# Four graph layers on one core: the hops' weights applied to the rows before the sweeps, in place of after them

## The chip, the core and the metric

The kernel runs on one core of one Trainium2 chip. The metric is the device time of one execution in microseconds; the kernel before has a median of 759.16 us over three runs (756.97 to 760.65). All work of a run is in one program: TensorE (PE, with its weight loads shown apart as PEld), VectorE (DVE), ScalarE (ACT), GpSimd (POOL) and SyncE (SP, which only issues transfers here).

## The reference

x is 4096 x 64, adj is a dense 4096 x 4096 float32 matrix (64 MB) that is mostly zero. Four layers are applied one after another, each as x = x + layer(h) with h = relu(layernorm(x)):

```
layer 0:  1 - 0.1 h - 0.01 sum(h * (adj @ h), axis=1)
layer 1:  two hops: for k in 0, 1:  y = tanh(concat([adj @ y, y], 1) @ W[k])      (y starts as h, W[k] is 128 x 64)
layer 2:  mask = adj != 0; rank = cumsum(mask, 1); only the last 100 nonzeros of a row count,
          each weighted with 0.5 ** (its distance from the end);  w @ (h @ weight) + bias
layer 3:  tanh([h, t] @ W1 + b1) @ W2 + b2 + adj @ (h B^T) - rowsum(adj) * (h B^T)
```

A hop's argument of tanh is `(adj @ y) @ Wa + y @ Wx`, with Wa and Wx the upper and lower 64 rows of W[k]. It equals `adj @ (y @ Wa) + y @ Wx`, so that Wa can be applied on either side of the product with adj.

## The kernel before

adj has to be walked five times: sweep L0 (layer 0), L1A and L1B (the two hops), L2 (layer 2) and L3 (layer 3). A sweep has 8 chunks of 512 output rows (`W`), and a chunk has 16 blocks b of 256 adj columns (`TQ` = 2 tiles of 128), so a block is 128 x 1024 float32. Blocks travel in pairs of 1 MB: pair k holds blocks 2k and 2k+1. Pairs 0 and 4 of every chunk (and pair 2 of chunk 4) are kept in SBUF (`cache`) after L0; the others go through four landing slots (`land`). SP issues the loads in program order on one queue; a load waits until every engine that reads the slot's last pair is done with it. L1A and L2 walk the chunks backwards (`ch`), so a sweep begins with the chunk whose pairs are still in the slots.

In L0, L1A, L1B and L3 the two tiles of a block are multiplied as two 64-column halves into `accA` (L1157), with the transposed layer input as the weights: `X[0]` in L0, L1B, L3, and `X[1]` in L1A. The accumulated chunk is thus 2 x 64 rows (two partial sums, one above the other) by 512. In L0, DVE also makes the mask of each block (L979) and PE counts the nonzeros of each tile per output row (`count`, L1172), because L2 needs for every tile the number of nonzeros behind it. In L1A and L1B, DVE adds blocks into `totals` (L957, L961) for the row sums of layer 3, on the blocks in `TOTALS`. In L2 the masks go through a triangle matmul (L1189), ACT and, in block 6, DVE turn the result into weights (L484, L482), and PE multiplies them with the rows (L1200).

The rest of the work of a chunk (its epilogue, in numbered stages) is put between the blocks of the next chunk. Each engine runs the same loop: block b, then the stages whose place is b (`stages_after`). Places come from `STAGES_L1B`, `ROW_STAGES`, and `QUICK` for the first chunk of a sweep; in L0 and L1A stage b//2 stands at odd b. All queues are in order: a stage that waits holds up everything behind it on its engine. What the change touches:

- Epilogue of a hop (L1A, L1B): stage 0 transposes the four tiles of the hop's own rows (PE L1047, ACT L705 to `rowsT`); stage 1 copies `accA` to `accS` (ACT L739), and PE multiplies `rowsT` by Wx (L1081, `wx0`, `wx1`) and `accS` by Wa (L1085, `wagg0`, `wagg1`) into `nat`; stage 3 takes the tanh from PSUM (ACT L745 to `X[0]`, or L749 to `natS`).
- L1B's epilogue then goes on as the others do: rows added (DVE L927), the norm (DVE L841, L842, L847, L848, POOL L641, L634, L644, DVE L860), a transpose of the normed rows `hS` (PE L1047), and layer 2's product (L1106). PE also adds up `totals` (L1074).
- L0's epilogue: join of the two halves (L1093), row products on DVE (L885, L887), the new x (L893, L896), the norm into `X[1]` (stage 7, L860).
- Counts and left-over weights in L0: a tile's last row (`LAST` = 127) is left out of the triangle and is handled apart. ACT copies the upper half of the counts (L785), DVE adds the lower (L908) and fits in the last rows of adj (L913), which SP has loaded (`left_adjacency`, L515, issued behind the eight loads of the next chunk); ACT makes the weights (L792) and stores both.

Of the kernel before, what the change touches and what calls it, by code (L numbers as in the profile page):

```python
# [15 lines left out]
P = 128  # L16
N = 4096
D = 64
# [120 lines left out]
for _name, _n in (("wagg0", D), ("wx0", P), ("wagg1", D), ("wx1", P), ("l2w", P), ("bT", P), ("w1t", 2),  # L139
                  ("b1", 2), ("t", 1), ("bias", D), ("ident", P), ("join", D), ("ones", 1), ("full", 1),  # L140
                  ("w1", 256), ("w2", 2 * D), ("b2", D)):
    COLS[_name] = (_at, _at + _n)
    _at += _n
# [23 lines left out]
def tr_no(p, c, i=0):  # L167

    return {L1A: c, L1B: 8 + 2 * c + i, L2: 24 + c, L3: 32 + c}[p]
# [13 lines left out]
def totalled_no(p, c, b):  # L183
# [3 lines left out]
    return (first - 1) * c + at - 1 if p == L1A else (first - 1) * NC + second * c + at  # L187

# [29 lines left out]
def evac_no(c, b):  # L218

    on_dve = sum(k in EVAC_DVE for k in range(NQ))  # L220
    if b in EVAC_DVE:
# [5 lines left out]
HT_PE = {L1B: "turn", L2: 7}  # L227
HT_ACT = {L1B: "turned", L2: 7}
# [3 lines left out]
STAGES_L1B = {0: 1, 1: 3, 3: 7, 4: 8, 5: 10, "turn": 12, "turned": 13, 6: 15, 7: 15}  # L232

QUICK = {L1A: {0: 0, 1: 1, 3: 4, 4: 5, 5: 6, 6: 7, 7: 9}, L1B: {0: 0, 1: 1, 3: 4},
         L2: {3: 2, 4: 3, 5: 5, "turn": 8, "turned": 9, 6: 11, 7: 11, 8: 12},
# [5 lines left out]
def stages_after(p, c, b, before, before2):  # L241
# [9 lines left out]
    if p == L1B:  # L251
        return at_block({8: 2}, before2) if before2 and b == 2 else at_block(STAGES_L1B, before)
    found = []
# [33 lines left out]
def gnn_kernel(nc, x_in, adj_in, left_in_d, wts_in, tri_in, out):  # L287
# [3 lines left out]
    left_d = nc.dram_tensor("left_weights", (NC, 2 * NT, W), U16, kind="Internal").ap()  # L291
    hT_d = nc.dram_tensor("rows_transposed", (NC, P, 2 * P), F32, kind="Internal").ap()
    counts_d = nc.dram_tensor("counts", (NC, 2 * NT, W), BF16, kind="Internal").ap()
# [3 lines left out]
    with ExitStack() as ctx:  # L297
# [17 lines left out]
        later = sb("later", [P, 4 * NT], BF16)  # L315
        loS = sb("loS", [2 * NT, P], F16)
        lowS = sb("lowS", [2 * NT, 2 * W], U16)
# [50 lines left out]
        sums_p = nat[:, CH:CH + 4]  # L368
# [28 lines left out]
        left_rows, cleared = sem("left_rows"), sem("cleared")  # L397
# [64 lines left out]

        def rows4(t):
# [9 lines left out]
        def weights_out(eng, ops, c, b):  # L473
# [16 lines left out]
        def _(sp):  # L490
# [4 lines left out]
            tile_counts = counts_d.rearrange("c (t k) w -> c t k w", k=2)  # L495

            def counts_for(g):
# [3 lines left out]
                else:  # L501
# [4 lines left out]
                             tile_counts[ch(L2, c), 4 * k:4 * k + 4, 0].rearrange("(o t) w -> o t w", o=1))\  # L506
                    .then_inc(counts_in[g % (MASKS // 2)], 16)

            def left_adjacency(c):

                if c:
                    sp.wait_ge(left_later, c)
                else:
                    sp.wait_ge(cleared, 1)
                sp.dma_start(loadjS[1:2 * NT:2, :], left_in_d[:, c * W:(c + 1) * W]).then_inc(left_adj, 16)  # L515
# [7 lines left out]
            def left_rows_of(c):  # L523

                sp.wait_ge(cleared, 1)
                sp.wait_ge(copy_used, copied_no(L1B, c, 1) + 1)
                for t in range(4 * c, 4 * c + 4):
                    sp.dma_start(loS[2 * t + 1:2 * t + 2, :], tile16(t)[LAST:P, :]).then_inc(left_rows, 16)
# [102 lines left out]
        def _(pool):  # L631
# [56 lines left out]
            nc.gpsimd.memset(loS[:, :], 0.0)  # L688
            nc.gpsimd.memset(loadjS, 0.0).then_inc(cleared, 1)
# [4 lines left out]
        def _(act):  # L694
# [12 lines left out]
            def epilogue(at, e):  # L707
# [11 lines left out]
                if at == 0 and p in (L1A, L1B):  # L719

                    act.wait_ge(tr_done, tr_no(p, c, 0) + 1)
# [584 lines left out]
```

## Time and profile before

| | |
|---|---|
| median of 3 runs | 759.16 us (756.97 to 760.65) |
| the profiled execution | 757.24 us |
| its span, first to last instruction | 755.4 us |
| around the span | 1.8 us |
| granted TensorE clock, mean | 0.995 |
| PE, DVE, ACT, POOL busy | 93%, 58%, 25%, 14% of the span |
| moved by DMA | 262.58 MB, mean 348 GB/s |
| PE on sweep blocks (L1157) | 499 us in 2048 instructions |

A float32 product shows as two matmul instructions, so a block is 4 instructions of L1157. The matmuls of a stretch overlap: the mean of one (601 ns) says less than the distance from the start of one row of the timeline to the start of the next. In the timeline a sweep's chunk can be told by the copy of `accA` (L739, in L2 L737), one for each chunk. By these copies L0 takes from about 20 to 184 us, L1A to 319, L1B to 460, L2 to 614 and L3 to the end.

### The profile page before, as it was taken

What the parts mean: (1) busy time and instruction counts of PE and PEld (TensorE: products, weight loads), DVE (VectorE), ACT (ScalarE), POOL (GpSimd) and SP (SyncE); (2) the same over time, 40 slices, a digit from 0 to 9 for tenths busy, and PEclk for the clock granted to TensorE, in tenths of its full rate; (3) what the DMA queues carried; (4) which work ended last, traced back from release to release, by engine and by line L of the source; (5) the groups of instructions that cost most, each with busy time, mean ns of one, the idle gap of its engine ahead of it and who ended that gap; (6) DMA issues with size and microseconds to landing.
All of it is one profiled execution on the core that took longest, in us unless ns stands there. A gap on an engine that the chain in (4) does not pass through costs nothing. (4 is left out here: it accounts for less than half of the span.)

```text
span 755.4 us, 10059 instructions
## 1 busy us (share of the span) xinstructions
PE 703.3 (93%) x3656; PEld 280.1 (37%) x3656; DVE 438.7 (58%) x757; ACT 191.0 (25%) x279; POOL 104.8 (14%) x126
## 2 busy tenths in 40 slices
PE   1899999998999999999999997899999999999997
PEld 0333333333333333444444443344444433333332
DVE  5776776777888877846666556577777730000000
ACT  2010111110100000101111114688888842000100
POOL 5011011111100000002221222011111121211210
PEclk9999999999999999999999999999999999999999
DMA  9999999996699999699998986699899849999994
GB/s 370 379 365 412 416 420 414 413 412 249 232 406 401 333 382 374 261 376 369 374 367 311 363 329 224 220 356 394 302 379 375 331 143 362 369 413 399 363 385 159
DMA packets 49680, 262.58 MB, mean 348 GB/s; under 512 B 6880, under 2 KB 18912, under 8 KB 19296
## 3 DMA queue, kind: packets, MB, share of 16 engines
q1 hardware_dynamic: 39136, 252.51, 85.9%
q10 hardware_dynamic: 10496, 9.44, 4.0%
q8 instruction: 29, 0.48, 0.2%
q14 instruction: 19, 0.16, 0.1%
HBM read 255.76 MB, written 6.16 MB: 347 GB/s over the span
## 5 line engine op out<-in xcount | busy, mean ns | idle before, releaser
L1157 PE MATMUL accA<-land,X 128*64 128x512 f32 x1504 | 364.7, 601 | 8.9 <-DMA land<-adj_blocks 7.3
L1157 PEld LDWEIGHTS accA<-land,X 128*64 128x64 f32 x1504 | 100.4, 137 | 185.6 <-issue 138.9
L979 DVE TENSOR_SCALAR uS<-land 128x1024 bf16<-128x1024 f32 (+1 forms) x188 | 126.9, 723 | 42.6 <-DMA land<-adj_blocks 36.7
L961 DVE TENSOR_TENSOR uS<-uS,land 128x512 f32<-128x512 f32 x186 | 130.6, 702 | 34.7 <-DMA land<-adj_blocks 25.1
L1157 PE MATMUL accA<-cache,X 128*64 128x512 f32 x544 | 134.3, 605 | 16.5 <-DVE X L1012 12.6
L484 ACT ACTIVATE wS<-spare 128x1024 uint16<-128x1024 f32 x120 | 115.3, 1031 | 18.8 <-PE spare L1189 18.0
L1189 PE MATMUL spare<-uS,triA 128*128 128x512 bf16 x256 | 76.4, 380 | 10.4 <-DMA uS<-counts 3.8
L641 POOL TENSOR_TENSOR hS<-tS 128x256 f32<-128x256 f32 x24 | 21.2, 883 | 422.4 <-DVE tS L842 422.4
L1200 PE MATMUL accA<-wS,X 128*128 128x512 bf16 x256 | 76.3, 380 | 0.0
L945 DVE TENSOR_TENSOR tS<-uS,nat 128x256 f32<-128x256 f32 x8 | 3.4, 421 | 123.8 <-PE nat L1089 123.8
L1157 PEld LDWEIGHTS accA<-cache,X 128*64 128x64 f32 x544 | 38.9, 139 | 91.7 <-issue 84.7
L705 ACT ACTIVATE rowsT<-tr 128x256 f32<-128x256 f32 x32 | 12.3, 383 | 202.5 <-PE tr L1047 202.4
L1172 PE MATMUL spare<-uS,later 128*64 128x512 bf16 x256 | 50.0, 383 | 4.8 <-DVE uS L979 4.8
L979 DVE TENSOR_SCALAR uS<-cache 128x1024 bf16<-128x1024 f32 (+1 forms) x68 | 44.1, 687 | 7.7 <-DMA cache<-adj_blocks 5.1
L739 ACT ACTIVATE accS<-accA 128x512 f32<-128x512 f32 x32 | 19.1, 597 | 115.5 <-PE accA L1157 106.9
L961 DVE TENSOR_TENSOR uS<-uS,cache 128x512 f32<-128x512 f32 x54 | 37.7, 699 | 3.4
L1189 PEld LDWEIGHTS spare<-uS,triA 128*128 128x128 bf16 x256 | 20.1, 99 | 45.5 <-issue 27.0
L1200 PEld LDWEIGHTS accA<-wS,X 128*128 128x128 f16 x256 | 24.9, 97 | 30.6 <-issue 0.7
L634 POOL TENSOR_TENSOR rstd<-var,power 128x4 f32<-128x4 f32 (+1 forms) x25 | 29.7, 1189 | 38.7 <-DVE var L848 38.7
L792 ACT ACTIVATE wS<-wS,wts 64x512 uint16<-64x512 bf16 x8 | 5.8, 722 | 109.6 <-DVE wS L913 109.6
L1172 PEld LDWEIGHTS spare<-uS,later 128*64 128x64 bf16 x256 | 15.4, 111 | 43.2 <-issue 26.0
L482 DVE TENSOR_SCALAR wS<-spare 128x1024 uint16<-128x1024 f32 x8 | 9.8, 1224 | 23.0 <-PE spare L1189 23.0
(85 smaller groups left out, 392.5 us busy)
## 6 DMA issues: line engine op xcount, KB each, us to landing
land<-adj_blocks SPq DMA_DIRECT2D x219, 1024.0 KB, 7.4
cache<-adj_blocks SPq DMA_DIRECT2D x17, 1024.0 KB, 13.6
xin<-x_rows ACTq DMA_DIRECT2D x32, 128.0 KB, 7.6
x_rows<-zS ACTq DMA_DIRECT2D x24, 128.0 KB, 5.8
cache<-x_rows SPq DMA_DIRECT2D x1, 1024.0 KB, 4.9
uS<-counts SPq DMA_DIRECT2D x64, 4.0 KB
out_rows<-zS ACTq DMA_DIRECT2D x8, 128.0 KB, 6.7
rows_transposed<-rowsT SPq DMA_DIRECT2D x7, 128.0 KB, 7.8
```

The source lines that it names most:

```text
L482: ops.tensor_scalar(w, of, 0.0, None, ALU.max).then_inc(w_ready_dve, 1)
L484: ops.activation(w, of, ACT.Relu).then_inc(w_ready, 1)
L634: nc.gpsimd.tensor_tensor(out[:, 0:ntile], of[:, 0:ntile], power[:, 0:ntile], ALU.pow)\
L641: nc.gpsimd.tensor_tensor(hS[:, :], tS[:, :], tS[:, :], ALU.mult).then_inc(rows_squared, 1)
L705: nc.scalar.activation(rowsT[:, :], tr[:, 0:2 * P], ACT.Copy).then_inc(tr_evac, 1)
L739: last = nc.scalar.activation(accS[:, :], accA[:, c % 2, :], ACT.Copy)
L961: nc.vector.tensor_tensor(total, total, of[:, i * W:(i + 1) * W], ALU.add)\
L979: nc.vector.tensor_scalar(masks(b)[0:rows, :], block_of(p, c, b)[0:rows, :], 0.0, None, ALU.not_equal)\
L1157: last = nc.tensor.matmul(accA[k * D:(k + 1) * D, c % 2, :], tile(X[p % 2], TQ * q + k), of[:, k * W:(k + 1) * W], start=(b == 0), stop=(b ...
L1172: last = nc.tensor.matmul(spare[k * D:(k + 1) * D, c % 2, :], later[:, 2 * (NT - t):2 * (2 * NT - t)], masks(b)[:, k * W:(k + 1) * W], sta ...
L1189: last = nc.tensor.matmul(spare[:, 2 * (b % 2) + k, :], triA[:, :], masks(b)[:, k * W:(k + 1) * W], start=True, stop=True)
L1200: last = nc.tensor.matmul(accA[:, c % 2, :], tile16(TQ * q + k), weights(n)[:, k * W:(k + 1) * W].bitcast(BF16), start=(b == 0 and k == 0) ...
```

## The change

1. A hop's weights are applied before its sweep. `wagg`, `wx` (64 and 128 columns) become one table `hop0`, `hop1` of [Wa, Wx]. After the norm of a chunk in L0 (and after the tanh in L1A) the new rows are transposed (stage "turn", PE; "turned", ACT) and multiplied by [Wa, Wx] (stage "hop", PE, 4 products with 64 rows of contraction and 128 columns, into banks 2 and 3 of `spare`). ACT copies y @ Wa to `X[1]` or `X[0]`, which the sweep multiplies with adj, and y @ Wx to `Z` (stage "hopped"); `Z` lies in the space of the layer-2 weights `wS`.
2. After a hop's sweep PE only transposes `accS` (4 transposes, as L3 does); DVE adds the two halves and `Z` (stage "added", 2 operations of 128x256), and ACT takes the tanh from SBUF (stage "tanh").
3. Counts: the count matmul keeps its two column halves. ACT copies all 128 partitions as bf16 (stage "part"), one matmul adds the halves ("stack"), DVE copies 32 rows ("counts"), ACT makes the left-over weights for 32 rows ("weights", with the counts' store), DVE multiplies them by `adj != 0` of the last rows ("left"), ACT stores them ("left out"). Both stores are 32 rows, where they were 64, and the zeroed buffers on POOL go.
4. Places: L0 and L1A have tables of their own, `STAGES_L0` and `STAGES_L1A`. Entering L1A, the norm of L0's last chunk stands at blocks 1 to 6 (it stood at 4 to 9), ahead of most of the adding of row sums.
5. The weights of layer 2 in the first four blocks wait until the part of `Z` that they overwrite has been read.

The core of the diff:

```
-def tr_no(p, c, i=0):
-
-    return {L1A: c, L1B: 8 + 2 * c + i, L2: 24 + c, L3: 32 + c}[p]
+def tr_no(p, c):
+
+    return {L0: c, L1A: 8 + c, L1B: 16 + c, L2: 24 + c}[p]
...
-QUICK = {L1A: {0: 0, 1: 1, 3: 4, 4: 5, 5: 6, 6: 7, 7: 9}, L1B: {0: 0, 1: 1, 3: 4},
-         L2: {3: 2, 4: 3, 5: 5, "turn": 8, "turned": 9, 6: 11, 7: 11, 8: 12},
+STAGES_L0 = {0: 1, 1: 2, "part": 3, 3: 5, "stack": 5, "counts": 6, 4: 7, 5: 8, "weights": 8, 6: 10, "left": 10, 7: 11,
+             "left out": 12, "turn": 13, "turned": 13, "hop": 14, "hopped": 15}
+STAGES_L1A = {1: 2, "added": 4, "tanh": 6, "turn": 8, "turned": 9, "hop": 11, "hopped": 13}
+STAGES_L1B = {0: 1, 1: 3, "added": 5, "tanh": 6, 3: 7, 4: 8, 5: 10, "turn": 12, "turned": 13, 6: 15, 7: 15}
+QUICK = {L1A: {0: 0, 1: 1, 3: 1, 4: 1, 5: 2, 6: 4, 7: 6, "turn": 10, "turned": 10, "hop": 11, "hopped": 12, "part": 13,
+               "stack": 14, "counts": 14, "weights": 14, "left": 15, "left out": 15},
+         L1B: {1: 1, "added": 2, "tanh": 3, "turn": 5, "turned": 5, "hop": 7, "hopped": 8},
+         L2: {"added": 0, "tanh": 0, 3: 2, 4: 3, 5: 5, "turn": 8, "turned": 9, 6: 11, 7: 11, 8: 12},
```

The new stage on PE:

```
+                if at == "hop":
+
+                    pe.wait_ge(tr_evac, tr_no(p, c) + 1)
+                    if hop_no(p, c):
+                        pe.wait_ge(hop_evac, 2 * hop_no(p, c))
+                    for t in (0, 2, 1, 3):
+                        half = (t // 2 * D, t // 2 * D + D)
+                        last = nc.tensor.matmul(spare[:, 2 + t // 2, t % 2 * P:(t % 2 + 1) * P],
+                                                rows_t(t % 2)[half[0]:half[1], :],
+                                                wt("hop0" if p == L0 else "hop1", rows=half), start=True, stop=True)
+                    last.then_inc(hop_done, 1)
```

The new stage "added" on DVE, and what waits there for the last rows of adj:

```
+                def hop_added():
+
+                    if tanh_no(p, c):
+                        dve.wait_ge(tanh_done, tanh_no(p, c))
+                    dve.wait_ge(nat_done, nat_no(p, c, 0) + 1)
+                    dve.wait_ge(hop_evac, 2 * hop_no(p - 1, ch(p - 1, ch(p, c))) + 2)
+                    parts = nat[:, :].rearrange("p (t h d) -> p h t d", h=2, d=D)
+                    L(nc.vector.tensor_tensor(rows4(tS), rows4(chunk(Z, ch(p, c))), parts[:, 0], ALU.add))
+                    nc.vector.tensor_tensor(rows4(tS), rows4(tS), parts[:, 1], ALU.add).then_inc(nat_evac, 1)
+
...
+                    if at == "left":
                         dve.wait_ge(left_adj, 16 * (c + 1))
-                        dve.wait_ge(count_ready, c + 1)
+                        dve.wait_ge(left_most, c + 1)
```

How the order of the instructions moves, at the three places that matter below. First PE, one chunk of L1B (the second hop), from the last blocks of one chunk to the middle of the next. `tr` holds transposes, `nat` what is to go back to rows. Before:

```order
L1106 MATMUL nat<-wts,rowsT 128x2x64 x2
L1157 MATMUL accA<-land,X 64x512 x4
L1047 MATMUL tr<-wts,X 64x128 x4
L1157 MATMUL accA<-land,X 64x512 x4
L1074 MATMUL nat<-wts,uS 128x1 x4
L1081 MATMUL nat<-wts,rowsT 128x2x64 x2
L1085 MATMUL nat<-wts,accS 128x64 x4
```

After the change:

```order
L1141 MATMUL nat<-wts,rowsT 128x2x64 x2
L1207 MATMUL accA<-land,X 64x512 x8
L1115 MATMUL tr<-wts,uS 128x1 x4
L1122 MATMUL nat<-wts,accS 128x128 x4
L1207 MATMUL accA<-land,X 64x512 x4
```

The transposes of the hop's rows (L1047) and the two products by weights (L1081, L1085) are gone from this place; four transposes of `accS` (L1122) are there.

Second DVE, in L0, the second half of a chunk (uS<-land and uS<-cache are the masks of blocks; the first row of each piece is the mask of block 10 or 12). Before, the work on the left-over weights (L908, L913) stands behind the mask of block 15, the last of the chunk:

```order
L847 TENSOR_REDUCE st<-hS 128x4 [waits rows_squared]
L848 TENSOR_SCALAR var<-st 128x4 [waits link]
L979 TENSOR_SCALAR uS<-land 128x1024 [waits counted,landed2] x2
L860 TENSOR_SCALAR X<-tS 128x256 [waits rows_scaled]
L908 TENSOR_TENSOR wS<-wS,spare 64x512 [waits counts_out,count_half]
L913 SCALAR_TENSOR_TENSOR wS<-wS 64x512 [waits left_made,count_ready,left_adj]
```

After the change:

```order
L873 TENSOR_REDUCE st<-hS 128x4 [waits rows_squared]
L874 TENSOR_SCALAR var<-st 128x4 [waits link]
L954 SCALAR_TENSOR_TENSOR countS<-lowS,rowsT 32x512 [waits left_out,left_most,left_adj]
L1024 TENSOR_SCALAR uS<-land 128x1024 [waits counted,landed0]
L886 TENSOR_SCALAR hS<-tS 128x256 [waits rows_scaled]
L1024 TENSOR_SCALAR uS<-land 128x1024 [waits counted,landed1] x2
L1024 TENSOR_SCALAR uS<-land 128x1024 [waits counted,landed2] x2
```

The operation that waits for the last rows of adj (`left_adj`) now stands ahead of the masks of blocks 11 to 15.

Third ACT at the first blocks of L2 (L484 and L513 make the weights of a block). Before:

```order
L705 ACTIVATE rowsT<-tr 128x256 [waits nat_done,tr_done]
L739 ACTIVATE accS<-accA 128x512 [waits nat_done,swept]
L484 ACTIVATE wS<-spare 128x1024 [waits tri_done] x3
L749 ACTIVATE natS<-nat 128x256 [waits copy_used,nat_done]
L484 ACTIVATE wS<-spare 128x1024 [waits tri_done]
```

After the change:

```order
L740 DMA xin<-x_rows 128x256 [waits rows_out,copy_used]
L755 ACTIVATE accS<-accA 128x512 [waits nat_done,swept]
L513 ACTIVATE wS<-spare 128x1024 [waits nat_evac,tri_done]
L767 ACTIVATE natS<-tS 128x256 [waits copy_used,nat_evac]
L513 ACTIVATE wS<-spare 128x1024 [waits nat_evac,tri_done] x3
```

The copy of transposed rows (L705) is gone from here, and the tanh (L749, now L767) stands behind the weights of one block, where it stood behind those of three.

## Rows read from the trace of the kernel before

**Rows 1.** The page, part 1: busy us (share of the span) xinstructions

```profile
PE 703.3 (93%) x3656; PEld 280.1 (37%) x3656; DVE 438.7 (58%) x757; ACT 191.0 (25%) x279; POOL 104.8 (14%) x126
```

**Rows 2.** Windows: us, PE, PEld, DVE, ACT, POOL, clock, DMA share, GB/s

```profile
101.20:122.50 21.30, 19.63 (x104) 6.93 (x104) 15.22 (x28) 2.35 (x5) 2.55 (x3) 1.00 1.02 414
...
372.10:390.00 17.90, 17.90 (x106) 8.10 (x104) 10.99 (x20) 1.89 (x6) 3.81 (x5) 1.00 0.96 355
```

**Rows 3.** Timeline of PE in L1B: start us, us, engine, line, tile

```profile
374.05 0.69 PE L1081 MATMUL nat<-wts,rowsT 128*128 128x128 f32 x4
374.58 1.00 PE L1085 MATMUL nat<-wts,accS 128*128 128x64 f32 x8
375.51 1.94 PE L1157 MATMUL accA<-land,X 128*64 128x512 f32 x8
...
388.81 0.61 PE L1047 MATMUL tr<-wts,X 128*64 128x128 f32 x8
389.25 1.89 PE L1157 MATMUL accA<-land,X 128*64 128x512 f32 x8
```

**Rows 4.** Timeline of PE in L3

```profile
686.03 1.14 PE L1120 MATMUL spare<-wS 64*128 64x256 f32 x8
...
688.11 0.66 PE L1089 MATMUL nat<-wts,accS 128*128 128x128 f32 x4
688.69 1.94 PE L1157 MATMUL accA<-land,X 128*64 128x512 f32 x8
```

**Rows 5.** Timeline of ACT: the copies of accA, L1B and L3

```profile
353.84 0.61 ACT L739 ACTIVATE accS<-accA 128x512 f32<-128x512 f32 x1
...
443.78 0.60 ACT L739 ACTIVATE accS<-accA 128x512 f32<-128x512 f32 x1
...
649.96 0.60 ACT L739 ACTIVATE accS<-accA 128x512 f32<-128x512 f32 x1 [11.02 <-PE accA L1157]
...
750.82 0.60 ACT L739 ACTIVATE accS<-accA 128x512 f32<-128x512 f32 x1 [11.69 <-PE accA L1157]
```

**Rows 6.** SP's issue of the last rows of adj, and its time to landing

```profile
171.13 0.47 SPq L515 DMA_DIRECT2D wS<-adj_left  x1
...
DMA to landing us min/median/max: 10.3/10.3/10.3
```

**Rows 7.** Timeline of DVE in the last chunk of L0: masks of blocks 10, 11

```profile
175.79 1.29 DVE L979 TENSOR_SCALAR uS<-land 128x1024 bf16<-128x1024 f32 x2
```

**Rows 8.** DMA issues in a chunk of L0 (142:163) and of L3 (670:686)

```profile
land<-adj_blocks SPq DMA_DIRECT2D x6, 1024.0 KB, 11.3
...
land<-adj_blocks SPq DMA_DIRECT2D x6, 1024.0 KB, 8.0
```

**Rows 9.** Timeline of PE from L0 to the end of L1A's first chunk

```profile
183.57 1.89 PE L1157 MATMUL accA<-land,X 128*64 128x512 f32 x8
187.32 1.08 PE L1093 MATMUL nat<-wts,accS 128*128 128x64 f32 x8 [1.86 <-ACT accS L739]
...
195.22 7.04 PE L1157 MATMUL accA<-land,X 128*64 128x512 f32 x32
202.09 1.89 PE L1157 MATMUL accA<-cache,X 128*64 128x512 f32 x8
```

**Rows 10.** Windows after that wait: columns as in rows 2

```profile
190.00:192.00 2.00, 2.00 (x8) 0.73 (x6) 1.90 (x5) 0.00 (x0) 0.00 (x0) 0.50 0.27 92
```

**Rows 11.** Timeline of DVE: the last norm of L0, first and last operation

```profile
188.84 0.43 DVE L885 TENSOR_TENSOR tS<-X,natS 128x256 f32<-128x256 f32 x1 [0.60 <-ACT natS L749]
...
197.44 0.29 DVE L860 TENSOR_SCALAR X<-tS 128x256 f32<-128x256 f32 x1 [0.86 <-POOL tS L644]
```

**Rows 12.** Timelines of PE and DVE in the first chunk of L2

```profile
461.61 1.03 PE L1189 MATMUL spare<-uS,triA 128*128 128x512 bf16 x4
...
472.92 1.01 PE L1189 MATMUL spare<-uS,triA 128*128 128x512 bf16 x2 [3.62 <-DVE wS L482]
...
465.41 0.16 DVE L921 TENSOR_SCALAR rowsum<-nat 128x4 f32<-128x4 f32 x1 [4.92 <-ACT natS L749]
```

More of the change, by code:

```diff
@@ L187, in totalled_no, with hop_no, tanh_no @@
     return (first - 1) * c + at - 1 if p == L1A else (first - 1) * NC + second * c + at
+def hop_no(p, c):
+    return {L0: c, L1A: 8 + c}[p]
+def tanh_no(p, c):
+    return {L1A: c, L1B: 8 + c}[p]
 def row_no(p, c):
@@ L252, in stages_after @@
         return at_block({8: 2}, before2) if before2 and b == 2 else at_block(STAGES_L1B, before)
+    if p in (L0, L1A):
+        return at_block(STAGES_L0 if p == L0 else STAGES_L1A, before) if before else []
     found = []
@@ L741, in epilogue @@
                 if at == {L2: 2, L3: None}.get(p, 3):
[L742 to L746 removed]
+                    if p in (L0, L2):
+                        act.wait_ge(nat_done, nat_no(p, c, 0) + 1)
                         if copied_no(p, c):
                             act.wait_ge(copy_used, copied_no(p, c))
[L749 to L750 removed]
+                        nc.scalar.activation(natS[:, :], nat[:, 0:CH], ACT.Copy).then_inc(nat_evac, 1)
+                if at == "tanh":
+                    act.wait_ge(nat_evac, nat_no(p, c, 0) + 1)
+                    if p == L1B:
+                        act.wait_ge(copy_used, copied_no(p, c))
+                    nc.scalar.activation((hS if p == L1A else natS)[:, :], tS[:, :], ACT.Tanh).then_inc(tanh_done, 1)
+                if at == "hopped":
+                    act.wait_ge(hop_done, hop_no(p, c) + 1)
+                    for of, to in ((0, X[1] if p == L0 else X[0]), (1, Z)):
+                        nc.scalar.activation(chunk(to, ch(p, c)).rearrange("p (b t d) -> p b t d", b=2, d=D),
+                                             hop_out(of), ACT.Copy).then_inc(hop_evac, 1)
                 if at == HT_ACT.get(p, None):
@@ L754, in epilogue @@
                         act.wait_ge(hT_out, 16 * c)
-                    act.wait_ge(tr_done, tr_no(p, c, 1 if p == L1B else 0) + 1)
+                    act.wait_ge(tr_done, tr_no(p, c) + 1)
+                    if p in (L0, L1A):
+                        act.wait_ge(left_made, min(c + 1, NC - 1) if p == L0 else NC)
                     rows_transposed()
@@ L1052, in epilogue @@
                 p, c = e
-                if at == 0 and p in (L1A, L1B):
-                    tr_free(tr_no(p, c, 0))
-                    transposed(lambda j: tile(X[p % 2], 4 * ch(p, c) + j))
                 if p == L2 and at in ("join0", "join1") or p == L2 and c == NC - 1 and at == 1:
@@ L1286 @@
     put("ones", np.ones((P, 1), np.float32))
-    put("full", np.full((P, 1), NEIGH * BIT, np.float32))
+    put("full", np.full((P, 1), (NEIGH + 1) * BIT, np.float32))
     i, j = np.arange(P)[:, None], np.arange(P)[None, :]
```

170 lines of the change are left out of this document (83 added, 87 removed).

## The prediction

> **What bounds the kernel now.** I read the page first: PE is busy for 93% of the span, DVE for 58%, ACT for 25% [rows 1]. So each sweep is limited by PE or by the loads that it eats, and the windows by chunk tell which. In L0 a chunk takes 21.3 us with PE idle for 1.7 of them and DMA full at 414 GB/s: L0 goes at the pace of the loads. In L1B a chunk takes 17.9 us, PE has no gap at all, and DMA moves 355 GB/s, less than it has shown it can: L1B goes at the pace of PE [rows 2]. What is added to PE is thus free in L0 up to 1.7 us per chunk; what is taken from PE counts in L1B until the loads bind. The timelines at the borders between sweeps show where PE stands still: 1.86 us entering L1A [rows 9], with a granted clock of 0.50 some microseconds later [rows 10], and 3.62 us in L2's first chunk [rows 12].
>
> **L1B, per chunk.** Costs on PE are distances between starts. Removed: the transposes of the hop's rows, 0.44 us (388.81 to 389.25), the product by Wx, 0.53 (374.05 to 374.58), the product by Wa, 0.93 (374.58 to 375.51) [rows 3]: 1.90 us. Added: four transposes of `accS`, which L3 does already, 0.58 us (688.11 to 688.69) [rows 4]. Net -1.32 us. A chunk of L1B now takes (443.78 - 353.84) / 5 = 17.99 us, and would take 16.67 if PE alone counted. The nearest measure of the other bound is L3: nearly the same PE work, six loads of 1 MB and three transfers of 128 KB, (750.82 - 649.96) / 6 = 16.81 us [rows 5]; L1B has one transfer of 128 KB fewer. I take 16.75 for L1B, between the two, so 1.2 us saved. L1B's first chunk trades 1.90 us of L1A's old epilogue for the new one of L1A (below) and gains 0.1; its last chunk has few loads and gains the full 1.3. The seven chunks: 6 x 1.2 + 1.3 = 8.5 us saved. DVE's two new adds (0.42 us each, as its other operations of this size) and ACT's copies lie beside PE: DVE is busy for 11 of 17.9 us there [rows 2]. Without that cover they would cost 0.85 us per chunk.
>
> **L1A, per chunk.** Removed 1.90 us, added 0.58 (transposes of `accS`), 0.44 (transposes of the tanh's rows) and the hop's own products. Those have no row of their own. Nearest above: the hidden layer's products in L3, also with 64 rows of contraction and 128 columns of weights, but 256 columns wide, 1.14 us [rows 4]. Nearest below: the transposes, as many instructions of the same width, 0.44 us [rows 3]. I take 0.75, since the weights, which must be loaded in both, are as wide as in the row above. Sum +1.77 - 1.90 = -0.1 us; DVE gets 0.85 us more, and loads wait for DVE in this sweep. I count L1A as unchanged (-1 to +3 us over the sweep).
>
> By the Trainium skill (TensorEngine Tiling (Array Packing), Key Properties) a change of tiling mode drains TensorE. The sweeps run in column halves and the hop in row halves, so each hop is entered and left through a drain. The row of the hidden layer includes its own drains, and taken whole it would make the hop 0.4 us dearer, 3 us over L1A.
>
> **L0.** PE gets 0.44 + 0.75 us for turn and hop and about 0.3 for the stack: 1.5 of the 1.7 us that are free [rows 2]. Stores fall by 64 KB of about 8.8 MB per chunk, 0.15 us, 1 us in all. But DVE now waits for the last rows of adj behind block 10. In the last chunk SP issues them at 171.13, and they land 10.3 us later, at 181.4 [rows 6], since they stand behind the loads on SP's queue. DVE is done with block 10 at about 176.4 (two masks from 175.79) [rows 7]. So the mask of block 11 comes some 5 us later, in this chunk and in the like ones before it. Queued behind it are the norm and the masks of blocks 12 to 15, for which PE's counts wait, and both hold landing slots. While loads are the bound this costs little: a load now takes 11.3 us from issue to landing, so that four slots' worth are under way; held 3 us longer they take about 8, which is L3's figure [rows 8], at a like rate. I give it +2 us over seven chunks for slots that come back later, and with the saving +1 (bounds -1 and +8, the latter 1.2 us per chunk).
>
> **L0 to L1A.** Here the loads have ended and the 5 us show. Before, L1A begins at 183.57 [rows 9]. After, in the same clock: landing 181.4, the operation of 0.68 us and a mask of 0.69 make 182.8; then PE has the counts of blocks 11 to 15 and the sweeps of 13 to 15 (4 x 0.21 + 3 x 0.86, the last count after them), turn and hop with their switches (1.4), and is done at about 187.8: 4.2 us later. In L1A's first chunk PE gains the wait of 1.86 us for `accS` (ACT is free now when the sweep ends) and up to 1.8 us that the low clock took [rows 9, 10], and gets 1.5 us of turn, hop and stack. It also gets a wait: the norm on DVE took 8.6 us from natS on (188.84 to 197.7) with row sums between [rows 11]; with the norm put ahead it will still take about 8.5, since DVE and POOL alternate, and starts some 3 us into the chunk. PE reaches the turn behind block 10 after 11 x 0.86 + 1 = 10.5 us, the norm ends near 12: 1.4 us of wait. The chunk has 64 instructions of 0.215 us (6.87 us for 32) [rows 9], so 13.7, with 1.0 of joins, 0.2, 1.5, switches 0.3, wait 1.4: 18.1 us, against 202.09 - 183.57 = 18.5. DVE, which got less done by then, ends its row sums a little later still. Border: +4 us (-2 to +6).
>
> **L1B to L2.** PE comes to the first triangle (461.61) about 1.0 us sooner: `accS` no longer waits for the copy of the transposed rows, and 1.3 us of work are gone. DVE now waits 4.92 us for the tanh, up to 465.41, because it stands behind three weight copies on ACT [rows 12]. With the adds done at about 461.6 and one weight copy ahead of it, the tanh ends at about 463.0: 2.5 us sooner. The norm, the weights of block 6 on DVE and the triangle of block 8 (472.92) move up by the same 2.5 us. What is late next is the same chain, shifted. -2.5 us, -4 if the shorter stall keeps the clock up. L2's later chunks and L3 are untouched.
>
> **Sum**, against the profiled execution (757.24 us, 1.8 of them around its span): -8.5 (L1B), -0.1, +1 (L0), +4 (border), 0 (L1A), -2.5 (L2) = -6 us: 751.2. The median of the runs is 1.9 us above the profiled execution, so I forecast 753 us.
>
> **Rivals.**
> - The wait on the last rows of adj is no wait: they land with the reduced queue well before, or PE catches up. For it: the shorter the queue, the sooner a small transfer lands. Against it: they stand behind pair 7 in program order, which is needed at 18 us of a chunk's 21.3. Then the border costs nothing and may even gain the 1.86 us and the clock: 753 - 6 = 747. Chance 0.22.
> - L1B runs into the loads at once, and drains around the hops cost PE in L1A. For it: DMA share 0.96 in L1B [rows 2]. Against it: L3's 16.81 us. With 17.2 us for L1B (355 GB/s at a share of 0.96 is 370 at 1.00, by which the 6.55 MB of six loads and two transfers of 128 KB take 17.7; I take the middle of that and 16.67) the gain is 6 instead of 8.5, and L1A loses 3: 758. Chance 0.22.
> - It gets slower: in L0 the stall on DVE closes a loop. The slots of blocks 10 and on come back later, pair 7 is issued later, and the last rows behind it land later. PE work from the wait to the next issue of pair 7 is some 13.5 us (four blocks, turn, hop, six blocks with join), and the loop holds the chunk as soon as the landing takes over 7.8 us, or as soon as the one long gap lowers PE's clock as in [rows 10]. At 1.5 us per chunk and the border at +5.5 us: 753 + 9.5 + 1.5 = 764. Chance 0.14.
> - The forecast itself: 0.42, its own range 749 to 757.
>
> **How the numbers follow.** A change of about 0.5% (3.8 us) is what a measurement of this kernel can tell from none; 755.4 is the border. Faster: 0.36 of the forecast, all of the first rival, a little of the second: 0.60. Same: the rest of the forecast and most of the second: 0.25. Slower: 0.15. The range reaches down to the first rival with its clock gain, 745, and up to short of the third, 761.
>
> **What will show it.** Copies of `accA` in L1B 16.7 us apart, in L1A as now. The hop's products 0.75 us. In L0 an idle of 4 to 5 us on DVE ahead of the "left" operation, put down to adj_left, chunks of 21.3 to 21.6 us, and L1A beginning some 5 us late. PE's wait for DVE in L2's first chunk 1.5 to 2 us in place of 3.62. I am wrong if "left" shows no wait, if chunks of L0 grow past 22.3 us, or if L1B stays above 17.2.

## The result: slower by 0.8%, with the profile after

The changed kernel takes 765.51 us (median of eight runs) against 761.18 us for the kernel before in the same set of runs, a ratio of 1.0076, 95% interval 1.0051 to 1.0102. The ratios here compare the fast runs of a set only, and they are estimates that differ from the quotient of the two medians beside them (1.0057 for this pair). `changed_again`, the same kernel in the set of the first experiments, gave 767.37 against 760.17 us, 1.0116 (1.0081 to 1.0150). The forecast was 753 us and faster. The profiled execution took 767.67 us with a span of 765.8 us, 10.4 us more than before. The first part of its page shows PE with 1.9 us more of busy time [rows 1], so on balance most of the 10.4 us is waiting:

```profile
PE 705.2 (92%) x3664; PEld 274.3 (36%) x3664; DVE 452.0 (59%) x789; ACT 203.6 (27%) x311; POOL 104.3 (14%) x124
```

The starts of the sweeps on PE, read from both timelines, say where it went:

| stretch | before, us | after, us | difference | forecast |
|---|---|---|---|---|
| start to the first block of L1A | 183.57 | 196.63 | +13.1 | +1 in L0 and +4.2 at its end |
| L1A | 133.6 | 137.9 | +4.3 | -0.5 |
| L1B, to the first triangle of L2 | 144.4 | 138.2 | -6.2 | -9.5 |
| L2, to the first copy in L3 | 175.6 | 175.0 | -0.6 | -1.5 |
| L3 | 118.2 | 118.1 | -0.1 | 0 |

Two thirds of what the change was to give back in L1B came; L0 took twice as much. In L0 the chunks are longer, all but one. The windows of the changed kernel from copy to copy of `accA` (columns as in rows 2):

```profile
61.20:83.42 22.22, 20.27 (x123) 8.12 (x121) 15.00 (x29) 3.34 (x7) 2.62 (x3) 1.00 1.01 395
83.42:107.52 24.10, 21.96 (x123) 8.82 (x121) 15.42 (x30) 3.34 (x7) 2.62 (x3) 0.93 1.00 404
107.52:128.38 20.86, 20.36 (x124) 8.12 (x122) 14.23 (x28) 3.34 (x8) 3.11 (x3) 1.00 1.00 397
128.38:152.29 23.91, 21.95 (x123) 8.82 (x121) 15.36 (x29) 3.33 (x7) 2.61 (x3) 0.93 0.98 375
152.29:174.12 21.83, 20.27 (x124) 8.13 (x121) 14.64 (x28) 3.34 (x8) 2.62 (x3) 1.00 0.97 375
```

There are three kinds of chunk: one of 20.86 us, in which PE is nearly never idle; those of about 22 us, in which PE is busy for the same 20.3 us and idle for nearly 2; and those of 24 us, in which the granted clock of 0.93 is added, and with it 1.7 us more of busy time. Before, a chunk was 21.3 us at 414 GB/s [rows 2]; here the 22 and 24 us ones move 375 to 404. So L0 no longer goes at the pace of the loads. The waits of DVE and of PE between 57 and 186 us, as total, times and longest, say on what:

```profile
PE spare L1222 <- DVE uS L1024: 8.1, 5, 2.1
...
DVE tS L923 <- ACT natS L762: 16.4, 6, 3.8
DVE countS L948 <- PE spare L1157: 10.0, 6, 1.7
DVE countS L954 <- DMA lowS<-adj_left: 8.2, 4, 2.3
DVE uS L1024 <- DMA land<-adj_blocks: 5.4, 4, 1.7
```

Before, PE did not wait for DVE at all in this stretch, and DVE waited for hardly anything but loads (27.8 us for `land`, 5.1 for `cache`, and 2.6 us in two short waits for PE and POOL). Now DVE's waits for loads have shrunk to 5.4 us for `land` and 1.2 for `cache`, which is to say that it is the late one, and PE's counts (L1222) wait 8.1 us for its masks (L1024). One turn of it in the timelines of DVE, of PE and of SP's queue:

```profile
144.45 0.68 DVE L954 SCALAR_TENSOR_TENSOR countS<-lowS,rowsT 32x512 uint16<-32x512 f32 x1 [2.10 <-DMA lowS<-adj_left]
145.16 0.69 DVE L1024 TENSOR_SCALAR uS<-land 128x1024 bf16<-128x1024 f32 x1
...
145.91 0.41 PE L1222 MATMUL spare<-uS,later 128*64 128x512 bf16 x2 [1.96 <-DVE uS L1024]
146.15 1.72 PE L1207 MATMUL accA<-land,X 128*64 128x512 f32 x4
...
136.38 0.42 SPq L540 DMA_DIRECT2D lowS<-adj_left  x1
...
160.30 0.42 SPq L540 DMA_DIRECT2D lowS<-adj_left  x1
```

SP asks for the last rows of adj at 136.38, they land at 144.4, DVE has stood for 2.10 us, the mask behind the product (L954) is late, PE waits 1.96 us for it, and the next four matmuls, which mostly take 1.03 us, take 1.72. The next request of SP, which stands behind loads whose slots PE and DVE give back, goes out at 160.30.

### The profile page after: what moved, and what is told of

Same layout as the page of the kernel before. It is cut to its first block and busy times, and to the rows that moved or that the text cites. A ratio compares the mean times of both kernels' runs of the same rounds, so it can differ in the third digit from the quotient of the medians.

```text
span 765.8 us, 10173 instructions
## 1 busy us (share of the span) xinstructions
PE 705.2 (92%) x3664; PEld 274.3 (36%) x3664; DVE 452.0 (59%) x789; ACT 203.6 (27%) x311; POOL 104.3 (14%) x124
## 5 line engine op out<-in xcount | busy, mean ns | idle before, releaser
L1207 PE MATMUL accA<-land,X 128*64 128x512 f32 x1504 | 369.7, 607 | 7.3 <-DMA land<-adj_blocks 7.1
L1006 DVE TENSOR_TENSOR uS<-uS,land 128x512 f32<-128x512 f32 x186 | 133.0, 715 | 29.3 <-DMA land<-adj_blocks 20.5
L1024 DVE TENSOR_SCALAR uS<-land 128x1024 bf16<-128x1024 f32 (+1 forms) x188 | 127.5, 721 | 18.9 <-DMA land<-adj_blocks 12.5
L513 ACT ACTIVATE wS<-spare 128x1024 uint16<-128x1024 f32 x120 | 115.1, 1031 | 16.8 <-PE spare L1239 16.0
L665 POOL TENSOR_TENSOR hS<-tS 128x256 f32<-128x256 f32 x24 | 23.5, 979 | 460.0 <-DVE tS L868 460.0
L1222 PE MATMUL spare<-uS,later 128*64 128x512 bf16 x256 | 50.6, 391 | 16.7 <-DVE uS L1024 16.7
L1024 DVE TENSOR_SCALAR uS<-cache 128x1024 bf16<-128x1024 f32 (+1 forms) x68 | 44.6, 686 | 1.8 <-DMA cache<-adj_blocks 1.2
L1222 PEld LDWEIGHTS spare<-uS,later 128*64 128x64 bf16 x256 | 15.3, 113 | 61.9 <-DVE uS L1024 37.8
L1092 PE MATMUL tr<-wts,hS 128*64 128x128 f32 x256 | 21.5, 290 | 4.4 <-DVE hS L886 4.1
L1092 PEld LDWEIGHTS tr<-wts,hS 128*64 128x64 f32 x256 | 16.4, 145 | 21.9 <-issue 21.6
```

What stands on the lines that cost most here:

```text
L513: ops.activation(w, of, ACT.Relu).then_inc(w_ready, 1)
L665: nc.gpsimd.tensor_tensor(hS[:, :], tS[:, :], tS[:, :], ALU.mult).then_inc(rows_squared, 1)
L1006: nc.vector.tensor_tensor(total, total, of[:, i * W:(i + 1) * W], ALU.add)\
L1024: nc.vector.tensor_scalar(masks(b)[0:rows, :], block_of(p, c, b)[0:rows, :], 0.0, None, ALU.not_equal)\
L1092: last = nc.tensor.matmul(tr[half:half + D, (j % 2) * P:(j % 2 + 1) * P], of(j), wt("ident"), start=True, stop=True)
L1207: last = nc.tensor.matmul(accA[k * D:(k + 1) * D, c % 2, :], tile(X[p % 2], TQ * q + k), of[:, k * W:(k + 1) * W], start=(b == 0), stop=(b ...
```

## The experiments

The changed kernel was timed once more, unedited, beside the first three experiments as their measure:

> The changed kernel as it is, as the yardstick for the others of this call. It was 0.8% above the kernel before (about +6 us). Every theory expects the same again, 1.005 to 1.010.

Its 1.0116 is above, a little over the 1.005 to 1.010 expected, and its L0 shows the same: PE waits 9.1 us for DVE's masks between 57 and 186 us, DVE 9.5 us for the last rows of adj.

**The wait is a loop: the rows asked for three loads earlier, and one load later.** `left_early` moves SP's request from behind the eighth load of a chunk in L0 to behind the fifth; nothing else.

```diff
-                    for cc, k in L0_LOADS[c * PAIRS:(c + 1) * PAIRS]:
+                    for i, (cc, k) in enumerate(L0_LOADS[c * PAIRS:(c + 1) * PAIRS]):
+                        if c and i == 5:
+                            left_adjacency(c - 1)
...
-                    if c:
-                        left_adjacency(c - 1)
```

> One edit: in the first sweep SP issues the last rows of adj behind five of the chunk's eight loads, not behind all eight. Theory A (the wait of DVE for these rows, which stand last in the queue, closes a loop: landing, masks 11 to 15, PE, slots, pair 7, landing; its one long gap also lowers PE's clock): the wait on DVE vanishes, chunks of the first sweep fall from 22.5 to 21.3 to 21.6 us, the first hop begins 2 us sooner after the last load; 8 to 11 us less than the changed kernel, 3 to 5 us under the kernel before. Rival B (the 1.4 us of new PE work per chunk and the other new waits of DVE for PE hold the first sweep): the wait goes elsewhere, chunks stay above 22, at most 3 us gained.

Measured: 757.93 us, 0.9942 of before (0.9902 to 0.9982), 9.4 us below the changed kernel in the same set. The waits of PE and DVE in the same stretch, and two of its windows:

```profile
PE spare L1222 <- DVE uS L1024: 1.7, 4, 0.5
...
DVE uS L1024 <- DMA land<-adj_blocks: 15.7, 18, 1.4
...
DVE tS L923 <- ACT natS L762: 3.1, 3, 2.1
...
101.79:122.64 20.85, 20.35 (x124) 8.12 (x122) 14.79 (x28) 3.34 (x8) 3.11 (x3) 1.00 1.02 411
122.64:143.49 20.85, 20.48 (x123) 8.11 (x121) 14.97 (x29) 3.34 (x7) 3.11 (x3) 1.00 1.02 411
```

The product L954 has no wait left, DVE waits for loads again, its largest wait in the changed kernel (L923 for ACT, 16.4 us) has gone down to 3.1 with the other and so was a result of the loop, and every chunk up to 143.49 takes 20.85 us at a clock of 1.00 (later ones 21.3). L1A begins at 186.3 in place of 196.63.

`left_late` asks one load later, behind the first load of the chunk after, for six of the eight chunks.

```diff
-                    for cc, k in L0_LOADS[c * PAIRS:(c + 1) * PAIRS]:
+                    for i, (cc, k) in enumerate(L0_LOADS[c * PAIRS:(c + 1) * PAIRS]):
...
-                    if c:
-                        left_adjacency(c - 1)
+                        if c > 1 and i == 0:
+                            left_adjacency(c - 2)
+                    if c == NC - 1:
                         left_adjacency(c - 1)
```

> The opposite edit: the same transfer is issued one load of 1 MB later (behind pair 0 of the next chunk), for six of eight chunks. Theory A: every landing is about 2.5 us later, and a loop passes all of it on: chunks of 24.5 to 25 us, 12 to 15 us above the changed kernel. Rival B: the wait of DVE grows by 2.5 us but PE and the loads have room, under 4 us in all.

Measured: 779.03 us, 1.0265 (1.0213 to 1.0316), 11.7 us above the changed kernel, just under the 12 to 15 expected; its chunks are 24.5 us in the mean (66.43 to 189.11 in five). DVE and PE between 57 and 186 us (its lines are two further down, L956 is the product):

```profile
PE spare L1224 <- DVE uS L1026: 19.3, 6, 4.4
...
DVE countS L956 <- DMA lowS<-adj_left: 20.0, 6, 4.6
```

PE's wait is DVE's wait almost in full, 19.3 of 20.0 us. A stall on an engine that is busy for 59% of the changed kernel's span reached the engine that sets the pace almost without loss.

**DVE's product two blocks later.** `mask_behind` leaves SP alone and moves the product from block 10 to 12, ScalarE's store of it from 12 to 13.

```diff
-STAGES_L0 = {0: 1, 1: 2, "part": 3, 3: 5, "stack": 5, "counts": 6, 4: 7, 5: 8, "weights": 8, 6: 10, "left": 10, 7: 11,
-             "left out": 12, "turn": 13, "turned": 13, "hop": 14, "hopped": 15}
+STAGES_L0 = {0: 1, 1: 2, "part": 3, 3: 5, "stack": 5, "counts": 6, 4: 7, 5: 8, "weights": 8, 6: 10, 7: 11, "left": 12,
+             "left out": 13, "turn": 13, "turned": 13, "hop": 14, "hopped": 15}
```

> The changed kernel with VectorE's product for the left weights two blocks later in L0 (block 12 in place of 10, and ScalarE's store of it at 13 in place of 12); SyncE still asks for the last rows of adj behind all eight loads. Theory: what costs is that VectorE stands in that wait for 2.1 us with the masks of the next blocks queued behind it, and so counting, sweeping and the next loads; two blocks are some 2.6 us, so the rows have landed when it comes there, L0's chunks go from 22.5 us to about 20.9, and the time is that of left_early, 0.992 to 0.998 of before. Rival: it is the place of the transfer among the loads that costs; then nothing changes and the ratio stays at 1.008 to 1.015. A third: the transposes now wait for the product, since ScalarE's copy of them stands behind it, and the gain is only half.

Measured: 758.5 us, 0.9967 (0.9945 to 0.9988), in a set without the changed kernel. The waits in its L0:

```profile
PE spare L1222 <- DVE uS L1024: 3.4, 7, 0.7
...
DVE countS L954 <- DMA lowS<-adj_left: 3.0, 5, 1.3
```

The transfer is where it was among the loads and most of the loss is gone, so the transfer's place costs nothing by itself; what costs is what is queued behind DVE's wait. Some of the wait is left: with the loop looser the small transfer lands later, 9.9 us from issue in the median where it was 7.6 (below).

**The same edit on the kernel before.** `before_left_early` asks whether L0 was held before the change too.

> The kernel before with left_early's edit alone. Theory: before the change the wait for the last rows of adj had slack, since the hop's transposes did not stand behind it, so L0 keeps its 148 us from the copy of the first chunk to that of the last, and the time is 0.997 to 1.000 of before. Rival: the same loop slowed L0 before the change as well (its chunks took 21.2 to 22.3 us against 20.85 in left_early); then L0 shortens by 2 to 4 us and the time is 0.994 to 0.997 of before, as good as left_early itself, and moving the hops is worth nothing.

Measured: 762.04 us, 0.9992 (0.9959 to 1.0024). It changes nothing that shows, so the stall belongs to the change. Its L0, and that of `left_early` over the same six chunks:

```profile
59.70:188.16 128.46, 117.43 (x624) 41.51 (x620) 89.46 (x168) 13.78 (x25) 17.54 (x18) 1.00 0.96 388
...
60.08:186.12 126.04, 122.97 (x729) 48.35 (x726) 88.28 (x165) 20.04 (x42) 18.66 (x18) 1.00 0.98 395
```

With the stall out of both, L0 is shorter by 2.4 us with the change, although PE is busy there for 5.5 us more. That is not one trace's luck: over the same six chunks the four later kernels with the change and this edit take 126.1 to 126.9 us, the kernel before 128.9. Which part of the change gives it was not tried. The whole kernel gains about half a per cent (0.9942 against 0.9992), by intervals that overlap a little.

**Row sums out of L1A.** In L1A loads wait for DVE's adding of row sums. `sums_moved` moves two of ten blocks of each chunk to L1B.

```diff
-TOTALS = {L1A: (1, 2, 3, 4, 7, 9, 10, 11, 12, 15), L1B: (0, 5, 6, 8, 13, 14)}
+TOTALS = {L1A: (1, 2, 3, 7, 9, 10, 11, 15), L1B: (0, 4, 5, 6, 8, 12, 13, 14)}
```

> Two of the ten blocks per chunk whose row sums DVE adds in the first hop (4 and 12) are added in the second hop instead, 2.8 us of DVE work per chunk. Theory C (the first hop takes 0.55 us more per chunk because DVE got 0.85 us of adds and loads wait for DVE to free their slots): the first hop's chunks fall from 16.6 to about 16.0, the second hop's stay near 17.2 (it is held by its loads), 3 to 4 us gained over the changed kernel. Rival D (the first hop is held by the loads' own rate and by where the chunks' starts fall): no change in the first hop, and the second gets slower, 0 to +3 us.

Measured: 761.38 us, 1.0003 (0.9966 to 1.0040), 6.0 us below the changed kernel, more than expected. In its trace L1A is 131.3 us in place of 137.9, and L1B's chunks are 17.4 us, where they were 17.2, so I put some 4 us down to the edit (the L1A of single traces of the changed kernel differs by 2.5 us). Another 3 us stand in the first chunk of L2 (24.3 us from copy to copy, where the changed kernel had 27.2 and 27.6). They are not the edit's: `left_early`, without it, has 24.4, and `both_eased`, with it, 27.2. The granted clock goes with them, 1.00 in the two short ones, 0.94 in the long ones of the changed kernel and of `both_eased`, with 1.2 to 1.6 us more of PE's busy time; the rest of the 3 us is open. `both_eased` joins the edits of `left_early` and `sums_moved`.

> The changed kernel with two edits: in L0 the last rows of adj are asked for behind the fifth load of a chunk in place of the eighth (as in left_early), and blocks 4 and 12 of the column sums go from the first hop's sweep to the second (as in sums_moved). Theory: the two ease different places. left_early took 0.9942 of before and still had 112.5 us from the copy of L1A's first chunk to L1B's first, sums_moved had 110.7 there; so 2 us below left_early, 0.990 to 0.993 of before, and L1B stays at 17.1 us a chunk. Rival: the sums moved to L1B lengthen it by as much, since L1B's chunks wait for loads and the landing buffers are given back later: 0.994 as left_early. Either is faster than both kernels.

Measured: 752.61 us, 0.9892 (0.9852 to 0.9932): faster than both kernels. SP's waits between 225 and 315 us, in L1A, of the changed kernel and of this one:

```profile
SPq L648 <- DVE uS L1006: 55.3, 31, 4.0
SPq L649 <- PE accA L1207: 22.8, 27, 2.2
```

```profile
SPq L648 <- DVE uS L1006: 35.6, 19, 3.7
SPq L649 <- PE accA L1207: 34.4, 27, 2.4
```

A load is issued when its slot is free of both readers; in the changed kernel DVE was the later one 31 times, now 19 times, and PE's own waits for `land`, 2.8 us there, are gone. L1A takes 129.5 us, 8.4 less than in the changed kernel. By the copies of `accA` the four kernels with both edits have 129.9 to 132.1 us there and the two profiles without the change 130.8 and 132.4, so L1A is about as long as before the change.

**The store that waits in front of the copy.** At the start of L1A's second chunk PE waits 2.3 us in the changed kernel. As I read the timelines, ACT's store of the left weights waits for DVE's product, the product stands behind DVE's row sums, and the copy of `accA` stands behind that store. `left_out_late` is `both_eased` with the store one chunk later.

```diff
-"left": 15, "left out": 15}
+"left": 15}
...
+        return found + ([("left out", (L0, NC - 1))] if (p, c, b) == (L1A, 1, 3) else [])
```

> both_eased with one more edit: ScalarE's store of the left weights of L0's last chunk, which waits for VectorE's mask behind the row sums, is issued in the second chunk of L1A in place of the first. Theory: PE's wait of 2.3 us for the copy of the first chunk's sums, at the start of L1A's second chunk, is that store's wait ahead of it on ScalarE; it goes to under 1 us and the time falls by 1.5 to 2.5 us against both_eased. Rival: the sweep catches up in its next load-bound chunks (16.6 us where the content is 15.7), and the time is within 0.5 us of both_eased.

Measured: 756.3 us, 0.9898 (0.9853 to 0.9943), the same as `both_eased`. A miss of mine: with fewer row sums DVE comes to its product sooner, and PE's wait was already down to 0.4 us in `both_eased`. There was nothing left to gain, and so my reading of the 2.3 us stands untested by this edit; `sums_moved`, which shortens the row sums, takes the wait from 2.3 to 0.4.

**The norm's order, entering L1A.** `norm_behind` is `both_eased` with the norm at blocks 4 to 9 again.

```diff
-QUICK = {L1A: {0: 0, 1: 1, 3: 1, 4: 1, 5: 2, 6: 4, 7: 6, "turn": 10,
+QUICK = {L1A: {0: 0, 1: 1, 3: 4, 4: 5, 5: 6, 6: 7, 7: 9, "turn": 10,
```

> both_eased with the order of the norm in L1A's first chunk put back as it was before the change (stages 3 to 7 at blocks 4 to 9 in place of 1 to 6), all else as it is. Theory: the norm's end on VectorE then comes after more row sums, PE's wait ahead of the first chunk's transposes grows from 1.5 us to 3 to 6, and the hop behind it, so L1A's first chunk gets longer by 1.5 to 4 us, of which nothing is given back as PE sets the end there. Rival: loads bound L1A's first chunks and the row sums come earlier and give landing buffers back earlier, which gains what the wait costs: within 1 us of both_eased.

Measured: 753.26 us, 0.9871 (0.9830 to 0.9913), no different from `both_eased`. PE's wait ahead of the transposes, in `both_eased` and then in this one:

```profile
198.38 0.66 PE L1092 MATMUL tr<-wts,hS 128*64 128x128 f32 x8 [1.48 <-DVE hS L886]
```

```profile
198.82 0.66 PE L1092 MATMUL tr<-wts,hS 128*64 128x128 f32 x8 [1.78 <-DVE hS L886]
```

I expected 3 to 6 us and it is 0.3 more. PE waits for the norm's end 0.3 us longer and no more when more row sums stand between its steps, so this part of the change is worth nothing that shows.

**What sets L1B.** `turned_twice` is `both_eased` with the transposes of `hS` run twice in L1B, the second set over the first.

```diff
...
+                    if p == L1B:
+                        transposed(lambda j: tile(hS, j), False)
                     transposed(lambda j: tile(hS, j))
```

> both_eased with the four transposes of the rows run twice in each chunk of L1B (the first set is written over by the second), which is 0.44 us more of PE's work a chunk, 3.5 us in all. Theory that PE sets L1B's chunk (17.27 us in both_eased): they go to 17.7 us and the time grows by 3 to 3.5 us. Rival that the loads or VectorE set it: the chunks stay within 0.1 us of 17.27 and the time within 1 us.

Measured: 758.9 us, 0.9967 (0.9944 to 0.9990), some 6 us above `both_eased`. ACT's copies in L1B, four chunks apart, in `both_eased` and then here:

```profile
366.12 0.59 ACT L755 ACTIVATE accS<-accA 128x512 f32<-128x512 f32 x1
...
435.20 0.59 ACT L755 ACTIVATE accS<-accA 128x512 f32<-128x512 f32 x1
```

```profile
367.62 0.59 ACT L755 ACTIVATE accS<-accA 128x512 f32<-128x512 f32 x1
...
439.29 0.59 ACT L755 ACTIVATE accS<-accA 128x512 f32<-128x512 f32 x1
```

17.27 us a chunk became 17.92. Copy by copy the four are 18.44, 17.70, 17.83 and 17.70: three are 0.43 to 0.56 longer, for 0.44 us of added work, and the fourth holds two waits for loads:

```profile
378.10 1.94 PE L1210 MATMUL accA<-land,X 128*64 128x512 f32 x8 [0.44 <-DMA land<-adj_blocks]
380.57 1.08 PE L1210 MATMUL accA<-land,X 128*64 128x512 f32 x4 [0.53 <-DMA land<-adj_blocks]
```

So work added to PE counts there in full, and the loads are near enough to cost something now and then. The 6 us of the medians are more than the 3 to 3.5 expected and more than eight times 0.44; the rest is not explained.

## Why the prediction was wrong, step by step

**The step that failed is L0's, "+2 us over seven chunks for slots that come back later, and with the saving +1".** It took L0 as bound by loads and DVE's late masks as hidden by them. What the runs showed is the third rival, to which I gave 0.14 and 764 us: the loop. By the table this step and its sequel at the border are 7.9 of the 16.8 us that the forecast was off; L1A is 4.8, L1B 3.3 and L2 0.9 (below). That the rival's 764 lies so near the 765.5 measured is partly luck: it had some 16 us in L0 and at its end, where 13.1 were measured, and gains of 11 us elsewhere, where 2.6 were measured. The other half of the step held: with the loop out, `left_early`'s L0 shows that PE's added work there costs nothing. Two starts of the product without a clock dip between them:

```profile
167.97 0.68 DVE L954 SCALAR_TENSOR_TENSOR countS<-lowS,rowsT 32x512 uint16<-32x512 f32 x1 [1.69 <-DMA lowS<-adj_left]
...
190.26 0.68 DVE L954 SCALAR_TENSOR_TENSOR countS<-lowS,rowsT 32x512 uint16<-32x512 f32 x1 [2.16 <-DMA lowS<-adj_left]
```

SP's request between them stands at 182.12. The loop is 14.2 us from the product to the request (I had 13.5) and 8.1 us from the request to the product (I had put the threshold at 7.8): 22.3 us a turn, against 20.85 us of a chunk without it. I had every number of it in the rival and then priced the forecast by the other branch. The error was to reason that loads held longer land sooner, 11.3 us down to 8, "at a like rate". They did land sooner (7.5 us in this stretch), but between 110 and 170 us DMA moved 380 GB/s, where it moved 413 before: the late reader set the pace. The low clock of two of the chunks, 1.7 us each, is the other part that the rival named. `left_early` and `mask_behind` break the loop at two different places and both take 7 to 9 us off; `left_late` lengthens it and adds 11.7.

**The wait itself: 4 to 5 us forecast, 2.1 measured.** Here the transfer lands in 7.9 us (median). I computed the wait from rows of the kernel before, with their 10.3 us to landing [rows 6], and added it once at the end of the sweep, where it was paid six times in eight chunks, 12.1 us in all. That fewer loads stand ahead of the small transfer once DVE is late is my reading of it.

**L0 to L1A's first chunk.** L1A began 13.1 us later, and 10.3 of them are gone in `left_early`. The first chunk itself went as worked out: 18.3 us against 18.1, and PE's wait ahead of the transposes 1.49 us against 1.4. (The norm that I gave 8.6 us is 8.9 by its own rows, 188.84 to 197.73 [rows 11].)

**L1A, "unchanged (-1 to +3 us over the sweep)": +4.3.** The hop's products take 0.65 us from their start to the next row's, in L0 (150.52 to 151.17) as in L1A (230.58 to 231.23), and the transposes 0.4 to 0.5 as foreseen. The rows beside the hop are longer too:

```profile
150.21 0.38 PE L1222 MATMUL spare<-uS,later 128*64 128x512 bf16 x2
150.52 0.71 PE L1151 MATMUL spare<-wts,rowsT 64*128 64x128 f32 x8
151.17 1.08 PE L1207 MATMUL accA<-land,X 128*64 128x512 f32 x4
152.08 0.39 PE L1222 MATMUL spare<-uS,later 128*64 128x512 bf16 x2
```

The count ahead of it is 0.31 us from its start to the hop's, where 0.22 is usual, and the block behind it 0.91, where 0.86 is usual. A hop costs 0.80 us in all, and I took 0.75. By the Trainium skill (TensorEngine Tiling (Array Packing), Key Properties) a change of tiling mode drains TensorE; the trace has at most 0.14 us for the two changes around a hop, and not the 0.4 us more of my estimate. What I underrated is the clause "loads wait for DVE in this sweep". It got 0.85 us more a chunk on DVE, which already held the loads back, and the wait for the store ahead of the copy (2.3 us), which I did not see. With fewer row sums in L1A, `both_eased` has next to nothing of either (PE waits 0.4 us for the copy and none for loads between 225 and 315 us), and L1A is as long as before, which is what I had forecast for it.

**L1B, 8.5 us of saving by 16.75 us a chunk: 17.20 measured.** The mechanism was right, the term too large: copies at 368.42 and 454.41 give 17.20, so 0.79 us saved a chunk in place of 1.2. The second rival had 17.2. Two things are in it. A chunk without a wait for loads takes 16.89 us (403.17 to 420.06), where it took 17.93 before, so PE alone gives 1.04 and not 1.32. Most of what is missing stands ahead of the transposes of `hS`:

```profile
414.76 1.03 PE L1207 MATMUL accA<-land,X 128*64 128x512 f32 x4
415.87 0.66 PE L1092 MATMUL tr<-wts,hS 128*64 128x128 f32 x8
...
415.43 0.29 DVE L886 TENSOR_SCALAR hS<-tS 128x256 f32<-128x256 f32 x1 [1.81 <-POOL tS L668]
```

They start 1.11 us behind the block before them, where 0.86 is usual, just after DVE has written `hS` (415.43 to 415.72). The norm has the two new adds in front of it now; whether they are what makes it late was not tried. The rest are loads: PE waits 2.2 us for them in this sweep, and DMA moves 372 GB/s at a share of 1.00 (383 to 400 us), so both bounds lie close together, and L3 was too kind a neighbour. `turned_twice` shows that it is not the loads alone.

**L2's first chunk, -2.5: nothing of it.** PE's wait is 3.43 us, where 1.5 to 2 were forecast and 3.62 were before [rows 12]. DVE's path in the changed kernel, and ACT's request for the rows of x that L972 adds to:

```profile
473.49 0.41 DVE L897 TENSOR_TENSOR tS<-wS,nat 128x256 f32<-128x256 f32 x1
473.93 0.42 DVE L898 TENSOR_TENSOR tS<-tS,nat 128x256 f32<-128x256 f32 x1
474.27 1.29 DVE L1024 TENSOR_SCALAR uS<-land 127x1024 bf16<-127x1024 f32 x2
476.54 0.43 DVE L972 TENSOR_TENSOR zS<-xin,natS 128x256 f32<-128x256 f32 x1 [0.99 <-issue]
...
482.61 1.22 DVE L511 TENSOR_SCALAR wS<-spare 128x1024 uint16<-128x1024 f32 x1
...
471.08 0.34 ACTq L740 DMA_DIRECT2D xin<-x_rows  x1
...
DMA to landing us min/median/max: 5.4/5.4/5.4
```

The wait of 4.92 us for the tanh is gone as forecast, and the tanh is done at 474.8. But L972 starts at 476.54 all the same. Two masks stand ahead of it (to 475.56), and then a pause of 0.99 to which the profile gives no releaser. It ends when `xin` lands: asked for at 471.08 and landed 5.4 us later, at 476.5. In `left_early` the two fall together as well (456.39 and 5.3 us; L972 at 461.78). So what was next in line, by these traces, was a transfer that I had not looked at (no run moves it), and in ACT's queue its request stands behind the copy of layer 2's product (471.02). The first triangle is at 472.72, so DVE's weights come 9.9 us behind it, as before (461.61 and 471.55). The 1.0 us at the border itself did come, and is within L1B's row of the table: from layer 2's product to the first triangle PE took 3.51 us before (458.10 to 461.61) and takes 2.45 now (470.27 to 472.72).

## What to carry to other kernels

Where a transfer is issued behind loads that wait for slots, and its reader also frees those slots, write down the loop and add it up: if request, landing and the way back to the next request are longer than a chunk, that sum is the new chunk, whatever the shares of busy time say (here 22.3 us against 20.85, with DVE busy for 59%). Ask for a small transfer some loads ahead, or let its reader come to it later; either took 1.1% to 1.7% off the changed kernel here. When an engine gets more work in a sweep, look at which engine the loads' issues wait for, and move what can be moved off that one: with the two eased, the changed kernel was 1.1% faster than before (what moving the row sums would do for the kernel before was not tried), and with the first alone 0.6%.

## What I had not expected of the hardware

A transfer of 64 KB takes about as long as one of 1 MB issued beside it, and it rises and falls with those: between 110 and 170 us the medians from issue to landing are 7.6 us (`adj_left`) and 7.5 (`land`) in the changed kernel, 9.9 and 10.4 in `mask_behind`, and 12.5 and 10.7 in `left_early`, which is faster.

PE's granted clock fell after some waits and not after others as long. After the wait of 1.96 us at 145.91 four microseconds passed at 0.57 (first row), most of them at the lower of the two levels (0.50, which is 1.2 GHz), yet after those of 1.56 us at 169.42 and 2.03 at 191.72 the next matmuls took their usual 1.03 us. In L2's first chunk the changed kernel shows 0.57 (second row) behind a wait of 3.43 us, and `left_early` 1.00 (third row) behind 3.48:

```profile
146.00:150.00 4.00, 4.00 (x20) 1.87 (x22) 4.00 (x8) 0.38 (x1) 0.00 (x0) 0.57 0.99 395
484.00:486.00 2.00, 2.00 (x10) 0.81 (x12) 2.00 (x4) 1.02 (x1) 0.00 (x0) 0.57 0.44 171
```

```profile
469.20:471.20 2.00, 2.00 (x15) 0.93 (x16) 2.00 (x4) 1.02 (x1) 0.00 (x0) 1.00 0.03 6
```

Equal kernels differ by some microseconds from run to run, and the clock goes with it: `left_early`'s fastest run took 749.92 us at a mean granted clock of 0.996, its slowest 761.31 at 0.983. So a single profile's whole time can't carry a difference of 3 us.
